# A third PSUM buffer for the running sums of an eight-core sandwich kernel, and the step that finishes their statistics moved later on VectorE

## What is computed

```
x = x + _layernorm(_L0_attn_ref(_layernorm(x)))      # this first line is stage 1
x = x + _layernorm(_L0_ffn_ref(_layernorm(x), ...))  # stages 2 to 5

def _L0_attn_ref(x):          # mean over all positions up to and with t
    wei = softmax(where(tril == 0, -inf, 0))
    return einsum('ts,bsc->btc', wei, x)

def _L0_ffn_ref(x, ...):      # slot routing
    h = gelu(concat(x, slot_mean) @ w1 + b1)
    alpha = softmax of the 8 largest of (h @ w2 + b2) / (|tau| + 0.1), zero elsewhere
    S_new = GRU(alpha.T @ x / sum(alpha), S); y = layernorm(S_new + attention over the 64 slots)
    return (alpha @ (y @ wvp + bvp)) @ wo + bo
```

## Time and profile before

| | |
|---|---|
| median of 2 runs | 880.26 us (878.39 to 882.13) |
| the profiled execution | 879.94 us |
| its span, slowest core (core 3) | 878.4 us |
| spans of the eight cores | 870.0 to 878.4 us |
| mean granted TensorE clock | 0.609 to 0.617 |
| busy share of the span | PE 40%, DVE 37%, ACT 31%, POOL 17% |

### The profile page before, as it was taken

The page is one execution under the profiler, slowest core; times in us unless marked ns, Lnnn a source line. Parts: engine busy times, 40 slices in busy tenths (PEclk is TensorE's granted clock), DMA queues, the critical chain, the costliest instruction groups (busy, mean ns, idle before and its releaser), DMA issues.

```text
span 878.4 us, 7020 instructions; the slowest of 8 cores (870.0 to 878.4 us)
## 1 busy us (share of the span) xinstructions
PE 355.5 (40%) x1737; PEld 128.6 (15%) x1737; DVE 329.0 (37%) x1057; ACT 275.9 (31%) x344; POOL 144.9 (17%) x83
## 2 busy tenths in 40 slices
PE   0002354354344533778787214662121445423230
PEld 0001000000000000334443213221120111000000
DVE  0004514524524437564541102554002020488883
ACT  0001342342342343565673203871000110234332
POOL 2001242232232223000000001000000000154553
PEclk9999555555555555678998555555555557555555
DMA  7996989899990001000000453003551413033424
GB/s 194 250 271 182 118 97 118 98 119 102 115 119 0 0 1 37 0 1 1 1 1 1 80 112 61 1 1 72 107 114 36 114 49 107 25 130 158 168 119 191
DMA packets 69287, 76.29 MB, mean 87 GB/s; under 512 B 53216, under 2 KB 57312, under 8 KB 68640
## 3 DMA queue, kind: packets, MB, share of 16 engines
q0 software_dynamic: 4800, 22.25, 22.6%
q1 hardware_dynamic: 64448, 53.60, 21.2%
HBM read 68.72 MB, written 36.70 MB: 120 GB/s over the span
## 4 chain that ended last, share of the span: by engine, by line
PE 30%; DVE 27%; DMA 13%; issue 11%; ACT 9%; another core or an unknown queue 8%; DVEq 1%; ACTq 1%; POOLq 0%; POOL 0%; SPq 0%
DVE bn6x L192 11%; PE p_h L549 8%; DVE bn6c L192 5%; DMA whhT<-wih_bf 4%; DMA whhT<-whh_bf 4%; PE pcs L391 4%; DVE tmp L173 3%; PE pcs L399 3%; ACT anb L207 2%; PE ptot L403 2%; PE p_si L663 2%; PE pcs L395 2%; PE p_xt L579 1%; ACT x2bf L207 1%
## 5 line engine op out<-in xcount | busy, mean ns | idle before, releaser
L207 ACT ACTIVATE stat<-stat 128x2 f32<-128x2 f32 (+1 forms) x64 | 13.1, 204 | 302.7 <-DVE stat L184 300.9
L417 POOL TENSOR_TENSOR sb_x<-anb,sb_x 128x1024 f32<-128x1024 f32 x32 | 74.4, 2342 | 184.7 <-ACT anb L207 184.7
L391 PE MATMUL pcs<-x1b,s_tri 128*128 128x512 bf16 x64 | 32.7, 615 | 147.5 <-ACT anb L207 138.7
L192 DVE BATCH_NORM_STATS2 bn6c<-pcs 128x6 f32<-128x512 f32 x64 | 39.9, 685 | 134.0 <-PE pcs L399 128.6
L192 DVE BATCH_NORM_STATS2 bn6x<-sb_x 128x6 f32<-128x512 f32 x128 | 77.5, 678 | 0.0
L549 PE MATMUL p_h<-x3t,sb_w1a 128*128 128x512 bf16 x256 | 72.3, 453 | 12.2 <-DVE bn6x L192 8.0
L1156 POOL TENSOR_TENSOR sb_x<-fnb,sb_x 128x1024 f32<-128x1024 f32 x24 | 55.8, 2338 | 81.1 <-ACT fnb L207 81.1
L1094 PE MATMUL p_f<-sb_sv,sb_alphaT 64*128 64x512 bf16 x64 | 31.8, 608 | 70.1 <-ACT fnb L207 62.5
L207 ACT ACTIVATE x2bf<-sb_x,stat 128x1024 bf16<-128x1024 f32 x32 | 36.4, 1137 | 54.1 <-PE p_at L669 54.0
L207 ACT ACTIVATE x3b<-sb_x,stat 128x1024 bf16<-128x1024 f32 x32 | 37.9, 1233 | 46.1 <-DVE stat L173 27.1
L192 DVE BATCH_NORM_STATS2 bn6x<-p_f 128x6 f32<-128x512 f32 x64 | 39.8, 684 | 18.7 <-PE p_f L1094 18.4
(11 more groups left out here) (171 smaller groups left out, 509.6 us busy)
## 6 DMA issues: line engine op xcount, KB each, us to landing
sb_x<-x SPq DMA_DIRECT2D x8, 2048.0 KB, 39.1
out<-sb_x SPq DMA_DIRECT2D x8, 2048.0 KB, 6.6
whh_bf<-Whh POOLq DMA_DIRECT2D x1, 6144.0 KB, 61.8
wih_bf<-Wih POOLq DMA_DIRECT2D x1, 6144.0 KB, 119.7
wv_bf<-wv POOLq DMA_DIRECT2D x1, 2048.0 KB, 146.6
wvp_bf<-wvp POOLq DMA_DIRECT2D x1, 2048.0 KB, 164.8
wo_bf<-wo POOLq DMA_DIRECT2D x1, 2048.0 KB, 180.2
wst<-wv_bf SPq DMA_DIRECT2D x8, 256.0 KB, 2.6
```

The costliest lines, as they stand in the source:

```text
L192: return gv.emit([out], [a], lambda: v_.bn_stats(out, a))
L207: lambda: s_.activation(out, in_, func, bias=bias, scale=scale, accum_out=accum))
L391: ins = t.matmul(b[:, h * DH:(h + 1) * DH], c_tri[:], x1t[:, h * DH:(h + 1) * DH], start=True, stop=(j == 0))
L417: g.tensor_tensor(sb_x[:, j * D:(j + 1) * D], anb[:, (j % 3) * D:(j % 3 + 1) * D], sb_x[:, j * D:(j + 1) * D], op=OP.add).then_inc(sX2, 1)
```

## The change

There are three edits. First, the setup's two PSUM tensors are released after it, and a third buffer `pcs2` takes their two banks; `pcs[j % 2]` becomes `pcs[j % 3]` for writer and readers, and cs(j) waits for the readers of tile j-3, not j-2. Second, on VectorE, pC(pr-1) is no longer issued at the end of its own pair, but at the start of pair pr; where pr opens a group, that is behind the new group's bn6x, cA and pA. It has scratch columns of its own (44 and 45 of `tmp4`). Third, the setup's TensorE code now stands in a block of its own ahead of the allocation of `pcs2`, and TensorE waits for scT, which reads `p_init`, before the first sum.

```diff
--- before.py
+++ after.py
@@ -232,10 +232,10 @@
             VSTT(c1_, b1_, 0.25, b3_, OP.mult, OP.add)
             return VSTT(SC(kv, pj, n), b2_, -1.0 / 16.0, c1_, OP.mult, OP.add)
 
-        def post(ks, kb, kg, km, pj, n):
+        def post(ks, kb, kg, km, pj, n, sco=40):
             VRC(SC(ks, pj, n), SC(kg, pj, n))
-            VTS(tmp4[:, 40:40 + n], SC(km, pj, n), -0.25, None, OP.mult)
-            return VTT(SC(kb, pj, n), tmp4[:, 40:40 + n], SC(ks, pj, n), OP.mult)
+            VTS(tmp4[:, sco:sco + n], SC(km, pj, n), -0.25, None, OP.mult)
+            return VTT(SC(kb, pj, n), tmp4[:, sco:sco + n], SC(ks, pj, n), OP.mult)
 
         NG = NT // 4
         NPAIR = NT // 2
@@ -275,8 +275,9 @@
         pcs = [es1.enter_context(nc.psum_tensor("pcs0", [P, D], F32)),
                es1.enter_context(nc.psum_tensor("pcs1", [P, D], F32))]
         ptot = es1.enter_context(nc.psum_tensor("ptot", [1, D], F32))
-        p_init = es1.enter_context(nc.psum_tensor("p_init", [P, DH], F32))
-        p_ini_b = es1.enter_context(nc.psum_tensor("p_ini_b", [P, 8 * NS], BF16))
+        es1i = ExitStack()
+        p_init = es1i.enter_context(nc.psum_tensor("p_init", [P, DH], F32))
+        p_ini_b = es1i.enter_context(nc.psum_tensor("p_ini_b", [P, 8 * NS], BF16))
 
         @blk.gpsimd
         def _(g):
@@ -306,6 +307,32 @@
             val["vini"] = VTS(sb_ninv[:], sb_invt[:], -1.0, None, OP.mult)
             v.wait_ge(sINI, 2)
             val["scT"] = VTT(sb_cT[:], p_init[:, 8:12], sb_b1T[:], OP.add)
+
+        @blk.tensor
+        def _(t):
+            t.wait_ge(semGi, 64)
+            t.wait_ge(semC, 64)
+            for dc in range(8):
+                t.matmul(p_init[:, dc:dc + 1], sb_Sbf[:, dc * P:(dc + 1) * P],
+                         c_tri[0:NS, 127:128], start=True, stop=True)
+            for dc in range(8):
+                ins = t.transpose(p_ini_b[:, dc * NS:(dc + 1) * NS],
+                                  sb_Sbf[:, dc * P:(dc + 1) * P], c_eye[0:NS, 0:NS])
+            ins.then_inc(sINI, 1)
+            t.wait_ge(sSVG, V("vini", 0))
+            w1bv = sb_w1b[:].rearrange("p (c j) -> p c j", j=DH)
+            for qc in range(4):
+                for dc in range(8):
+                    ins = t.matmul(p_init[:, 8 + qc:9 + qc],
+                                   w1bv[:, dc, qc * P:(qc + 1) * P],
+                                   sb_smT[:, dc:dc + 1], start=(dc == 0), stop=(dc == 7))
+            ins.then_inc(sINI, 1)
+
+        es1i.close()
+        pcs.append(es1.enter_context(nc.psum_tensor("pcs2", [P, D], F32)))
+
+        @blk.vector
+        def _(v):
             v.wait_ge(semC, 64)
             for g in range(NG):
                 v.wait_ge(semX[g], 16)
@@ -316,13 +343,16 @@
                 v.wait_ge(sSSG, V(("sq1", g), 0))
                 val["pA", g] = post(SM_S1, SM_B1, SM_G1, SM_MX, 4 * g, 4)
                 for pr in (2 * g, 2 * g + 1):
+                    if pr >= 1:
+                        v.wait_ge(sSSG, V(("sq2", pr - 1), 0))
+                        val["pC", pr - 1] = post(SM_S2, SM_B2, SM_G2, SM_MC, 2 * (pr - 1), 2, sco=44)
                     v.wait_ge(sCS, 2 * pr + 2)
                     for j in (2 * pr, 2 * pr + 1):
-                        VBN(bn6c[:, j * 12:j * 12 + 6], pcs[j % 2][:, 0:DH])
-                        val["bn6c", pr] = VBN(bn6c[:, j * 12 + 6:j * 12 + 12], pcs[j % 2][:, DH:D])
+                        VBN(bn6c[:, j * 12:j * 12 + 6], pcs[j % 3][:, 0:DH])
+                        val["bn6c", pr] = VBN(bn6c[:, j * 12 + 6:j * 12 + 12], pcs[j % 3][:, DH:D])
                     val["cC", pr] = combine(SM_MC, SM_VC, bn6c, 2 * pr, 2, c_e2[:, 2 * pr:2 * pr + 2])
-                    v.wait_ge(sSSG, V(("sq2", pr), 0))
-                    val["pC", pr] = post(SM_S2, SM_B2, SM_G2, SM_MC, 2 * pr, 2)
+            v.wait_ge(sSSG, V(("sq2", NPAIR - 1), 0))
+            val["pC", NPAIR - 1] = post(SM_S2, SM_B2, SM_G2, SM_MC, 2 * (NPAIR - 1), 2, sco=44)
 
         @blk.scalar
         def _(sc):
@@ -356,35 +386,20 @@
                     if jj >= 3:
                         sc.wait_ge(sX2, jj - 2)
                     val["an", jj] = SACT(anb[:, (jj % 3) * D:(jj % 3 + 1) * D],
-                                         pcs[jj % 2][:], AF.Identity,
+                                         pcs[jj % 3][:], AF.Identity,
                                          bias=SC(SM_B2, jj), scale=SC(SM_S2, jj))
 
         @blk.tensor
         def _(t):
-            t.wait_ge(semGi, 64)
-            t.wait_ge(semC, 64)
-            for dc in range(8):
-                t.matmul(p_init[:, dc:dc + 1], sb_Sbf[:, dc * P:(dc + 1) * P],
-                         c_tri[0:NS, 127:128], start=True, stop=True)
-            for dc in range(8):
-                ins = t.transpose(p_ini_b[:, dc * NS:(dc + 1) * NS],
-                                  sb_Sbf[:, dc * P:(dc + 1) * P], c_eye[0:NS, 0:NS])
-            ins.then_inc(sINI, 1)
-            t.wait_ge(sSVG, V("vini", 0))
-            w1bv = sb_w1b[:].rearrange("p (c j) -> p c j", j=DH)
-            for qc in range(4):
-                for dc in range(8):
-                    ins = t.matmul(p_init[:, 8 + qc:9 + qc],
-                                   w1bv[:, dc, qc * P:(qc + 1) * P],
-                                   sb_smT[:, dc:dc + 1], start=(dc == 0), stop=(dc == 7))
-            ins.then_inc(sINI, 1)
+            t.wait_ge(sSVG, V("scT", 0))
             for j in range(NT):
                 t.wait_ge(sSSG, V(("x1", j), 0))
                 if j >= 2:
-                    t.wait_ge(sSVG, V(("bn6c", (j - 2) // 2), 0))
-                    t.wait_ge(sSSG, V(("an", j - 2), 0))
                     t.wait_ge(sSSG, V(("cv", j // 2 - 1), 0))
-                b = pcs[j % 2]
+                if j >= 3:
+                    t.wait_ge(sSVG, V(("bn6c", (j - 3) // 2), 0))
+                    t.wait_ge(sSSG, V(("an", j - 3), 0))
+                b = pcs[j % 3]
                 x1t = x1b[:, (j % 4) * D:(j % 4 + 1) * D]
                 x1p = x1b[:, ((j - 1) % 4) * D:((j - 1) % 4 + 1) * D]
                 for h in range(2):
```

## The result

The changed kernel takes 860.2 us (median of 9 runs, 858.57 to 863.11), beside 880.71 us for the kernel before (8 runs on the same chip): a ratio of 0.977, 95% interval 0.975 to 0.979. That is 20.5 us less, where 20.55 us less were forecast (859.4 us). The profiled execution took 858.64 us, the span of its slowest core (core 5) is 857.1 us.

What follows compares the result with a forecast made beforehand. It took TensorE and VectorE taking turns in stage 1 as the bound. The third buffer's 14.25 us plus 6.30 us for the moved pC, 20.55 us off 879.94, gave 859.4 us, range 850 to 866 us.

Steps and rivals of the forecast that it cites:

- The ring: Stage 1: TensorE waits 138.7 us for ScalarE's an, VectorE 128.6 us for TensorE's sums; the engines take turns.
- The third buffer: Stage 1: TensorE waits for x1, not an; 0.95 us in each of 15 intervals, 14.25 us, between 13.1 and 18.0.
- What is late next: Stage 1, a pair's second tile: its inputs are ready 1.0 us early, so TensorE's 5.80 us stay unbroken.
- pC behind the group's statistics: VectorE at seven group boundaries: bn6x starts 0.90 us earlier, 6.30 us in all, between 5.8 and 7.0.
- The sum: Whole kernel: 14.25 + 6.30 = 20.55 us off 879.94 gives 859.4 us; intervals 12.35 us ordinary, 18.42 boundary.
- half of the clock case: TensorE's clock at 2.4 GHz in half of stage 1's intervals: 844 us.
- the worse stage 2: Stage 2's blocks about 0.9 us slower by a worse clock: 7.4 us come back, 866.8 us.
- Rival 1, the clock: Stage 1: TensorE's clock rises to 2.4 GHz; in every interval another 30 us less, 829 us; chance 0.07.
- Rival 2: Stage 2 runs at a worse clock: 7.4 us come back, 866.8 us; chance 0.06.
- Rival 3: Stage 1: GpSimd's additions hold VectorE's TENSOR_TENSORs by a port lock, 2.32 us an interval, 894 us; chance 0.02.
- Rival 4: Stage 1: another wait makes the buffer's gain nil, leaving 873.6 us, or 880; chance 0.06.

Runs made afterwards that it cites:

- e3: The changed kernel with TensorE's waits before a tile reordered: cv, bn6c and an first, x1 last; 0.974 of the kernel before, 857.4 us.
- e9: The changed kernel with the three satisfied waits behind x1 (cv, bn6c, an) written a second time; 0.987 of the kernel before, 868.19 us.
- e2: The kernel before, with two buffers, and only pC moved as in the change; 0.991 of the kernel before, 872.3 us.
- c_after_again: The changed kernel unaltered, run again on the same chip beside e9; 0.978 of the kernel before, 860.37 us.
- e4: The changed kernel with the next group's input statistics made in VectorE's wait for the odd pair's sums, sq1 ahead of sq2; 0.930, 819.1 us.
- e6: The changed kernel with ScalarE making both x1 and the carry copy ahead of sq2 at ordinary intervals, TensorE's last waits adapted; 0.944, 831.2 us.
- e7: The changed kernel with e6's ScalarE order at all intervals and the input statistics spread over the intervals; 0.878 of the kernel before, 773.4 us.
- e8: e7 with two buffers in place of three, and the waits of two buffers; 0.927 of the kernel before, 816.2 us.
- e5: e4 with e3's order of TensorE's waits; 0.928 of the kernel before, 816.9 us.

## Why the prediction was right

**The bound.** The ring was read rightly: both waits changed as said, and what lies behind stage 1 kept its length to 1.0 us.

**The third buffer.** The term was 15 x 0.95 = 14.25 us. It measured 0.87 us an ordinary interval, so 13.1 us, the lower of the two bounds. That bound came from extending one satisfied wait's 0.11 us to three (0.48 us expected, 0.46 measured); I took a value above it without a row that spoke for it. e3 and e9 show that each satisfied wait costs what the bound took, 0.11 us.

**What is late next.** Both waits of the second tile stayed hidden, with the matmuls 2.85 us apart as before.

**pC behind the group's statistics.** The term was 7 x 0.90 = 6.30 us; e2's boundary intervals show 0.90. Cover for pC was put at 0.46 us or more; it is 0.92, since pC does not wait for its square root there.

**The sum.** 13.1 + 6.3 = 19.4 us by these intervals. The trace has 20.0 us from first to last bn6c. Some boundaries were shorter still: 18.22 to 18.35 us where TensorE's clock rose at the end of its stretch, in place of 18.49. The first interval gained 1.11 us, since only one satisfied wait stands behind x1(2). Against that, the kernel before already had an ordinary interval of 12.87 us with the clock up. So two slightly wrong sizes, 1.1 us too much for the buffer and nothing for the clock, cancelled in part. That the medians then differ by the forecast 20.5 us is luck, since single executions of the changed kernel differ by 4.5 us. The range, 850 to 866 us, does not reach what it was said to reach: half of the clock case is 844 us, the worse stage 2 866.8.

**Rival 1, the clock.** It did not take over, but its sign appeared: the prediction names a granted clock clearly above 0.52 in stage 1. Before it was 0.51 or 0.52 on each of the eight cores; in the changed kernel it was 0.54 on the slowest core and 0.54 to 0.64 on all, in c_after_again too. It bought little. Much of the raised clock fell on pauses and on matmuls into `ptot`, for which bn6c does not wait: on the slowest core the interval from 207.04 to 219.46 had a granted clock of 0.62 and still took 12.42 us. Even on core 3, at 0.64, an interval was at most 0.4 us shorter than 12.42 us. The intervals at the low clock give 249.0 - 19.4 = 229.6 us from first to last bn6c, and the eight cores took 227.9 to 228.9, so I estimate the clock's part at 1 to 2 us of the 30 that the rival foresaw. The rule of the Trainium skill that the prediction cites ("TensorE: Matmul & The Clock Gate", What's actually happening), that activity releases the throttle, points the right way, and the size does not follow from it.

**Rival 2** did not show: the rest took 540.4 us against 539.4. **Rival 3** did not act in the change (159 ns), for want of overlap; its lock was shown in e4, where it cost 0.18 us an interval and not 2.3. **Rival 4** is out by the wait rows.

**What the prediction left unsaid.** It took ScalarE's order as given. The third buffer removed only 0.9 us of an interval of 13.3 because x1 and the carry copy stood behind sq2, and the input statistics stood at the boundary. e6 takes a further 3.3 us off an ordinary interval (12.42 to 9.10), and e7 9.3 us off a boundary one (18.43 on average to 9.10). e8 shows which part needs the third buffer: with two, the boundary falls to 11.97 us all the same, the ordinary interval only to 12.64.

## What to carry to other kernels

When one more buffer removes a wait, look at what else ends just before it: in an in-order queue, inputs placed behind an instruction that waits for the other engine keep the engines taking turns. Here e7's order, of ScalarE's queue and of the statistics, was worth 64.5 us with two buffers, and it turned the third buffer's 12 us into 43. So look at the order before you spend memory on a buffer, and look at the buffer again behind it. Put the wait that will be satisfied last at the end of a list of waits (0.32 us an interval here). Place statistics into another engine's turn, but keep their TENSOR_TENSORs away from GpSimd's additions.

## What the runs showed of the hardware that was not expected

Each satisfied wait behind the deciding one costs TensorE 0.11 us before its next matmul (0.14, 0.24, 0.46 and 0.78 us with 0, 1, 3 and 6 of them).

In e4 and e5 a small TENSOR_TENSOR of VectorE that starts during an addition of GpSimd ends with that addition, after 2.05 us in place of 0.15. In e4 one that is issued on the seam of two additions takes its usual 0.17 us.

The granted clock of a window and the speed of the matmuls in it do not always go together. In e7 the windows of 83 to 225 us show 1.00 on core 0 and 0.52 on core 1:

```profile
83.00:225.00 142.00, 113.50 (x239) 16.11 (x240) 94.98 (x351) 85.75 (x95) 69.04 (x30) 1.00 1.00 111
```

```profile
83.00:225.00 142.00, 112.13 (x240) 16.01 (x238) 95.56 (x352) 86.39 (x96) 67.89 (x31) 0.52 1.01 111
```

The same matmuls with the carry row took 616 ns on core 0 and 607 ns on core 1 on average, and the intervals are the same. What core 0's 1.00 means stays open; no run was made for it. In other places the matmuls did become faster, as at the end of this stretch of the changed kernel (first the even tile's two matmuls into `ptot`, then the odd tile's):

```profile
203.29 1.01 PE L418 MATMUL ptot<-x1b,s_tri 128*1 128x512 bf16 x2
...
206.87 0.59 PE L418 MATMUL ptot<-x1b,s_tri 128*1 128x512 bf16 x2
```

Where the matmuls ahead of bn6c did so too, the interval was shorter by up to 0.4 us.
